# Graph layer over an 8192 x 8192 matrix: the cells for the row sums of stripe s+1 loaded among the pieces of stripe s, and a later column step

## What is computed

```python
h = jnp.maximum(_layernorm(x, axis=-1), 0.0)
A_hat = adj + jnp.eye(N)
d_inv_sqrt = jnp.sum(A_hat, axis=1) ** (-0.5)
A_norm = d_inv_sqrt[:, None] * A_hat * d_inv_sqrt[None, :]
out = x + relu(A_norm @ (h @ W.T))
```

## Time and profile before

| | |
|---|---|
| median of 3 runs | 1205.84 us (1203.95 to 1207.55) |
| span of the profiled execution | 1237.8 us |
| time of the profiled execution apart from its span | none is listed |
| PE / DVE / ACT busy | 983.2 / 802.4 / 586.5 us |
| moved by DMA | 391.81 MB, mean 317 GB/s |
| mean granted TensorE clock | 0.909 of full |

### The profile page before, as it was taken

How to read it: one execution, slowest core, us unless ns; L and a number is a source line. 1 busy time by engine, 2 the same in 40 slices (tenths; PEclk the granted TensorE clock), 3 DMA queues, 4 the chain that set the end, 5 groups by cost and what they waited for, 6 DMA issues and landing times.

```text
span 1237.8 us, 9242 instructions
## 1 busy us (share of the span) xinstructions
PE 983.2 (79%) x2365; PEld 451.8 (36%) x2365; DVE 802.4 (65%) x965; ACT 586.5 (47%) x1735; POOL 52.6 (4%) x61
## 2 busy tenths in 40 slices
PE   0633346566687788796597999999999999899997
PEld 0631122222233333342243444444444444344443
DVE  5342233444476566575485888888888888778775
ACT  2797587776384637145254451724715653010011
POOL 3000000000000000000000000000000000010001
PEclk9767668678889899998798999999999999999999
DMA  9989999999999999999999999999999997999993
GB/s 301 380 320 309 392 398 362 365 369 347 362 349 343 362 337 322 314 256 274 281 291 278 329 332 360 323 276 333 309 325 320 314 271 215 271 271 348 337 328 88
DMA packets 275204, 391.81 MB, mean 317 GB/s; under 512 B 10832, under 2 KB 252624, under 8 KB 275152
## 3 DMA queue, kind: packets, MB, share of 16 engines
q1 hardware_dynamic: 137648, 195.65, 51.3%
q10 hardware_dynamic: 137504, 195.58, 50.5%
HBM read 386.99 MB, written 4.19 MB: 316 GB/s over the span
## 4 chain that ended last, share of the span: by engine, by line
PE 37%; DMA 8%; ACT 6%; ACTq 3%; DVE 1%; issue 0%; POOLq 0%; SPq 0%; DVEq 0%
PE bank L485 36%; DMA slot<-in_adj_dram 8%; ACT junk L540 6%; ACTq L269 2%; DVE adjT L692 1%; ACTq L277 1%; PE pre L461 0%; ACTq L315 0%; DVE near L778 0%; ACT slot L530 0%; ACT near L558 0%; DVE part L677 0%; POOLq L175 0%; PE sums_bank L449 0%; ACTq L321 0%
## 5 line engine op out<-in xcount | busy, mean ns | idle before, releaser
L485 PE MATMUL bank<-adjT,support 128*128 128x512 f32 x2048 | 936.2, 618 | 152.1 <-DVE adjT L692 150.8
L692 DVE STREAM_TRANSPOSE adjT<-slot 128x1024 f32<-128x1024 f32 x450 | 546.5, 1233 | 268.8 <-DMA slot<-in_adj_dram 157.2
L485 PEld LDWEIGHTS bank<-adjT,support 128*128 128x128 f32 x2048 | 401.8, 199 | 664.6 <-issue 661.0
L540 ACT ACTIVATE junk<-slot 128x384 bf16<-128x384 f32 (+2 forms) x540 | 254.6, 473 | 196.1 <-issue 131.3
L530 ACT ACTIVATE slot<-slot 128x6144 f32<-128x6144 f32 (+11 forms) x64 | 191.8, 2998 | 250.3 <-issue 147.8
L558 ACT ACTIVATE near<-near,dinv 128x128 f32<-128x128 f32 x64 | 20.4, 390 | 177.9 <-issue 88.5
L540 ACT ACTIVATION_READ_ACCUMULATOR junk<-slot 128x1 f32 x540 | 100.8, 187 | 0.0
L692 DVE STREAM_TRANSPOSE adjT<-near 128x1024 f32<-128x1024 f32 x62 | 74.8, 1231 | 19.0 <-PE bank L485 19.0
L540 ACT ACTIVATE junk<-near 128x256 bf16<-128x256 f32 (+1 forms) x192 | 75.5, 394 | 2.8 <-ACT junk L540 2.8
L677 DVE TENSOR_REDUCE part<-slot 128x4 f32<-128x1536 f32 (+2 forms) x45 | 69.0, 1533 | 0.0
L407 POOL TENSOR_TENSOR dinv<-total,power 128x4 f32<-128x4 f32 x16 | 16.1, 1007 | 942.0 <-DVE total L746 942.0
(11 more groups left out here) (53 smaller groups left out, 179.1 us busy)
## 6 DMA issues: line engine op xcount, KB each, us to landing
slot<-in_adj_dram SPq DMA_DIRECT2D x118, 768.0 KB, 15.4
slot<-in_adj_dram ACTq DMA_DIRECT2D x118, 768.0 KB, 13.4
slot<-in_adj_dram ACTq DMA_DIRECT2D x56, 512.0 KB, 11.0
slot<-in_adj_dram SPq DMA_DIRECT2D x56, 512.0 KB, 12.0
slot<-in_adj_dram ACTq DMA_DIRECT2D x12, 1536.0 KB, 15.8
slot<-in_adj_dram SPq DMA_DIRECT2D x12, 1536.0 KB, 17.0
near<-in_adj_dram SPq DMA_DIRECT2D x30, 512.0 KB, 16.8
near<-in_adj_dram ACTq DMA_DIRECT2D x30, 512.0 KB, 15.2
```

Of the source, the lines that this page charges most:

```text
L485: ins = nc.tensor.matmul(bank[bank_of(g)][:], support[:, v * R + t, :], adjT[at % TURNS][:, r, :], start=(n == first_of[g] and t == 0), st ...
L540: nc.scalar.activation(junk[at % JUNKS][:, :n], cells[:, c, :], ACT.Copy, accum_out=part[u % 2][:, k, c:c + 1]).then_inc(junk_done, 1)
L692: nc.vector.transpose(adjT[at % TURNS][:].rearrange("p t (c i) -> p t c i", i=Q), half.rearrange("p c (t r) -> p t c r", r=Q)).then_inc(t_ ...
```

## The change

The four far pieces of stripe s+1 are no longer loaded at the head of stripe s+1. They are spread evenly over the pieces of stripe s: after the k-th of its own pieces (left, near, early), as many far pieces as make the share k of all. ACT sums them where they stand in the new list `stream[s]`. Three `far_sum` tiles replace two.

```diff
+    for u in range(NB):
+        stream[u], left[u], early[u] = [], [], []
+        if u == 0:
+            for piece_ in far_pieces(0):
+                place_piece(0, piece_)
+        own = [("left", u, v, n, 0, 0) for v, n in split(0, u)] + ["near"]
+        if u <= EARLY_TO:
+            own += [("again", i, u - MOST, MOST, 0, 0) for i in range(u - MOST - BAND - 1, -1, -MOST)]
+        ahead = far_pieces(u + 1)
+        done = 0
+        for k, piece_ in enumerate(own):
+            if piece_ == "near":
+                near_behind[len(landing) - 1] = u
+                stream[u].append("near")
+            else:
+                place_piece(u, piece_)
+            upto = len(ahead) * (k + 1) // len(own)
+            for piece_ in ahead[done:upto]:
+                place_piece(u, piece_)
+            done = upto
...
     for s in range(NB):
-        before = 0 if NB - 1 - s - BAND > 4 else min(FIRST, max(0, s - 1))
-        order += own[:before]
-        if s > 0:
-            column(s - 1)
-        order += own[before:]
+        lefts, behind = todo[s]
+        order += lefts[ready:]
+        following = todo[s + 1][0][:s] if s + 1 < NB else rest[:LEAD]
+        stripe_at[s] = len(order)
+        begun = behind[:LEAD]
+        ready = min(len(following), LEAD - len(begun))
+        order += begun + following[:ready]
+        column(s)
+        order += behind[LEAD:]
...
-        far_sum = [sb(f"far_sum{i}", [P, 2 * B]) for i in range(2)]
+        far_sum = [sb(f"far_sum{i}", [P, 2 * B]) for i in range(3)]
...
-                if m + AHEAD in last_piece:
-                    load_kept(act, (2, 3), last_piece[m + AHEAD])
+                if m + AHEAD in near_behind:
+                    load_kept(act, (2, 3), near_behind[m + AHEAD])
...
-            for s in range(NB + 1):
-                end = stripe_at[s + 1] if s < NB else len(order)
-                early = stripe_at[s] if s == 0 else min(column_at[s - 1], stripe_at[s] + 1)
-                for n in range(stripe_at[s], early):
-                    product(n)
-                if s > 0:
-                    fold_sums(s - 1)
+            for n in range(len(order)):
+                if folds < NB and n == min(stripe_at[folds] + 2, column_at[folds]):
+                    fold_sums(folds)
+                    folds += 1
+                product(n)
...
+            for s in range(NB):
+                fold_at.setdefault(min(stripe_at[s] + 2, column_at[s]), s)
+                totals_at.setdefault(min(stripe_at[s] + 3, column_at[s]), s)
+                scale_at.setdefault(min(stripe_at[s] + 4, column_at[s]), s)
```

More of the change, by code:

```diff
@@ L82, in gnn_kernel, with far_pieces @@
     landing = []
-    far, left, again, early = {}, {}, {}, {}
+    far, left, again, early, stream = {u: [] for u in range(NB)}, {}, {}, {}, {}
+    near_behind = {}
     next_cell = [u + BAND + 1 for u in range(FAR_ROWS)]
     middle = []
-    for u in range(NB):
+    def far_pieces(u):
         cells = NB - 1 - u - BAND
-        far[u] = []
         widths = [] if cells <= 0 else [cells] if cells <= MOST * B else [MOST * B, cells - MOST * B]
+        out_ = []
         for k, width in enumerate(widths):
@@ L91, in gnn_kernel @@
             per = min(B, MOST * B // width)
[L92 to L99, removed]
-        if u <= EARLY_TO:
[L101 to L105, removed]
+            out_ += [("far", u, bb, min(per, B - bb), NB - cells + k * MOST * B, width) for bb in range(0, B, per)]
@@ L128, in column, with cells_of @@
             order.append((i, s, None))
+    def cells_of(m):
+        u, v, n = landing[m][1:4]
+        return [(u, k, m) for k in range(v, v + n)]
+    todo = []
+    for u in range(NB):
+        lefts = [cell for m in left[u] for cell in cells_of(m)]
+        behind = [cell for m in early[u] for cell in cells_of(m)]
+        todo.append((lefts, behind))
+    rest = [cell for u in AGAIN_ROWS for m in again[u] for cell in cells_of(m)]
+    ready = 0
     for s in range(NB):
+        lefts, behind = todo[s]
+        order += lefts[ready:]
+        following = todo[s + 1][0][:s] if s + 1 < NB else rest[:LEAD]
         stripe_at[s] = len(order)
-        own = [(landing[m][1], v, m) for m in left[s] + early[s] for v in range(landing[m][2], landing[m][2] + landing[m][3])]
-        before = 0 if NB - 1 - s - BAND > 4 else min(FIRST, max(0, s - 1))
-        order += own[:before]
-        if s > 0:
-            column(s - 1)
-        order += own[before:]
[L138 to L142, removed]
+        begun = behind[:LEAD]
[3 more added lines that the diff above has]
+        order += behind[LEAD:]
+        if s + 1 == NB:
+            order += rest[ready:]
     place = {(u, v): n for n, (u, v, m) in enumerate(order)}
@@ L339, in done_by @@
             return sum(combined_at(k) + 1 < place[u, v + n - 1] for k in range(NB))
-        last_piece = {(far[u] + left[u])[-1]: u for u in range(NB)}
         @block.sync
@@ L487, in product @@
                     ins.then_inc(used, 1)
-            back = 0
-            for s in range(NB + 1):
-                end = stripe_at[s + 1] if s < NB else len(order)
-                early = stripe_at[s] if s == 0 else min(column_at[s - 1], stripe_at[s] + 1)
-                for n in range(stripe_at[s], early):
-                    product(n)
-                if s > 0:
-                    fold_sums(s - 1)
-                for n in range(early, end):
-                    product(n)
-                    if back < NB and n >= 4 + last_final(back):
-                        rows_back(back)
-                        back += 1
+            back = folds = 0
+            for n in range(len(order)):
[3 more added lines that the diff above has]
+                product(n)
+                if back < NB and n >= 4 + last_final(back):
+                    rows_back(back)
+                    back += 1
             while back < NB:
```

118 lines of the change are left out of this document (63 added, 55 removed).

## The result

The change costs 6%: median 1282.47 us over four executions (1272.1 to 1309.8) against 1206.69 over four of before (1203.95 to 1209.0), a ratio of 1.0607 [1.0539, 1.0675]. The execution of 1309.8 us counts as a slow one, and the ratio is taken without it. The direction was forecast; the size was +3.6 us and came out at +73 by the ratio, +76 by the medians.

A forecast was written before the change was run, and what follows sets the result against it. DMA was taken to bound the first phase, PE the last. Terms +19.2 - 6 - 6.9 - 2.7 = +3.6 us gave a span of 1241.4 from 1237.8, and a median of 1209.5, range 1190 to 1229.

The forecast's parts named there:

- the three reliefs: Stripes 10 and 11: no near-load wait (-6 us), two cells less behind the arrival (-6.9), no cold start (-2.7).
- Nothing is loaded less ... I cost it at nothing; what hides it is the full DMA.: Spreading far pieces loads the same bytes, so no cell reaches PE sooner; costed at nothing because DMA is full.
- my rivals: ACT as bound in stripes 6 to 8 (1224, 0.25); waits cost nothing (1190, 0.28); change does nothing (1206, 0.05).
- something comes back: Stripe 9's 271 GB/s stretch, named as where spreading could gain if full DMA did not hide it.
- The waits of ACT, the main term: ACT waits at near(3) to near(5) for late columns, DMA losing 2.6, 6.6 and 10 us: +19, bounds 8 and 34.
- The arrival at 675.40: End of DVE's wait for the load at stripe 11's start; said to set the end, with 155 cells behind it.
- The frame itself: After that arrival PE sets the time: 155 cells x 3.43 = 532 us, plus 30 us for restart, folds and tail.
- The wait of stripe 10: ACT's 9.2 us before the near load, behind column(9); its removal was forecast to give 6 us, bounds 0 and 9.2.
- The rest cost nothing: Third far_sum, moved folds, totals and fold_sums, and DVE's fold waits for ACT: nothing on the path.
- The second phase: From about slice 24 PE is full almost to the end, a cell costing it 3.43 us.
- ACT as the bound at 1224: Rival: ACT also becomes the bound in stripes 6 to 8, 5 us for each of three stripes; chance 0.25.

The follow-up runs named there:

- e1: Far pieces spread as in the change, but with the cell order of the kernel before: median 1361.22 us.
- e2: Cell order (late column) as in the change, but far pieces at the head of their own stripe as before: 1320.32 us, 1.0945.
- e18: e1 with two pieces in flight in place of three: 1271.86 us, 1.0519.
- e6: Loads alone, computation left out, in the changed kernel's spread load order, three pieces in flight: span 1170.3 us.
- e17: e6 with two pieces in flight in place of three: span 954.5 us.
- e4: The changed kernel with all near loads issued by GpSimd in place of SP and ACT: 1287.88 us, 1.0507.
- e3: The changed kernel, but up to stripe 6 only early cells, no left cells, may stand before the column: 1355.26 us, 1.1235.
- e11: e1 with a wait for all issued pieces to land in front of near(2) to near(10): 1279.53 us, 1.0598.
- e9: The kernel before, unchanged, profiled once more: 1204.63 us, span 1202.8.
- e12: The kernel before with one number changed, so that columns 9 and 10 stand at the head of their stripes: 1204.8 us, 0.9977.
- e8: Loads of the kernel before and its order up to column 8; from column 9 on the column behind up to five early cells: 1229.17 us, 1.0166.
- e13: The changed kernel up to column 8, with the order of the kernel before from column 9 on: median 1295.68 us (1257.58 to 1301.48).
- e10: e6 with a wait once a stripe, before the near load, until all issued pieces have landed: span 1041.0 us.
- e5: Loads alone, computation left out, in the load order of the kernel before, three pieces in flight: span 1077.3 us.

## Why the prediction was wrong

The sum failed in more than one term. The spans differ by 67.5 us where 3.6 were forecast, and the missing 64 divide as an account of the trace: 23 up to stripe 6, of which about 13 are slower packets and about 10 longer waits; 15.6 for the three reliefs, which did not come; 25 elsewhere, nearly all of it behind the start of stripe 8, costed at nothing. Of these the sizes are estimates; that the terms add up so is not shown, since e1 and e2 show that the two parts of the change do not add.

**The step that failed: "Nothing is loaded less ... I cost it at nothing; what hides it is the full DMA."** The byte count was right, and the conclusion took DMA's rate as a property of the piece (413, 346, 295 GB/s). It is one of the order and of how much is in flight as well. The spread order without the late columns costs 4 to 5% with two pieces in flight and about 155 us with three (e18, e1), and the loads without any computation show the fall with three and only a sag with two (e6, e17). None of my rivals had this mechanism, and no row of before shows it, except one that I passed over: stripe 9 with a share of 1.04 at 271 GB/s. I called it a place "where something comes back". It was the same thing, long packets, and asking what a busy DMA at 271 GB/s is doing would have raised the question.

**The waits of ACT, the main term.** The mechanism was right in kind: near(3), near(4) and near(5) waited as predicted, ACT idle before them for over 10 us, the rate below 250 behind it. Near(2), which the prediction does not follow at all, waited 18.4 us. The size was off twofold and outside the term's own bounds of 8 to 34.

| lag gained from (s,0) to (s+1,0) around near(s) | near(2) | near(3) | near(4) | near(5) | near(6) |
|---|---|---|---|---|---|
| predicted, us | 0 | 2.6 | 6.6 | 10 | 0 |
| measured, us | 3.4 | 8.3 | 11.3 | 16.9 | 2.3 |

The sum is 42.2 instead of 19.2. For 100 to 400 us the windows divide it: the rate is down by 13.6% (360 to 311), the share by 9.6% (1.04 to 0.94), and so the rest, some 4.4%, is slower packets. Of 300 us that is about 29 for a DMA without work and 13 for slower packets. So of the 23 us that were missing, about 10 are my arithmetic of the waits (near(2), costed at nothing, waited 18.4 us; near(5) 21.9), and 13 the term above. This division holds for the traces as they are; e4 shows that the 29 do not come back when the holes are filled. Against ACT's time the account also closes, as an estimate: it waits 76.7 us after and then issues in 1.55 each, 84.4 in all, where before it was held 37.7 us by five issues of 4.5 to 9.9 without a wait; the difference is 46.7, and the lag at (7,0) 44.1. What the Trainium skill (DMA: Bandwidth & Descriptors, Anatomy of one DMA) says, that the issuing sequencer does the waiting, is what these gaps show.

**Parts that do not add.** e2 puts the late column at +114 us and e1 the spread at +155; together they cost 75. The far pieces between near load and left piece shorten the wait (21.9 us at most, where e2 has 30.3), and the waits drain DMA once a stripe and keep its packets short. Taking them away (e3) costs 73 us; putting in idle ones (e11) gives 60 to 80. I had only the cost of a wait in the sum, not what DMA does after a pause.

**The reliefs, -6, -6.9 and -2.7, were not there; a new wait was.** The arrival at 675.40, on which all three stand, lies late by the disturbed part of that execution; its 32 us over the median were a warning that I explained and then did not heed, reading microseconds from inside the stretch that made them. The frame itself holds in e9: (11,0) is waited for 7.8 us and transposed at 641.6, and 641.6 + 532 + 30 is 1203.6 against a span of 1202.8. The wait of stripe 10 is there too, but it is not what makes that arrival late, since e12 takes it away for 2.8 us. And the late column brings in its own wait, which the prediction did not see: the last early cell now stands behind two column cells, its slot is released 6.9 us later, and the loads behind it wait (some 16 us in front of one issue of e8, 20 us in all for the kernel, 5 of them before stripe 8). I had followed what the near load waits for, but not what the other loads wait for when `order` moves. "The rest cost nothing" failed with it: the fold two cells behind the last left cell holds DVE for 9.1 and 6.0 us in stripes 10 and 11.

**The second phase.** PE is not hungry behind stripe 11 in either kernel, and the lag grows by only 7 us from there to the end, as the frame of the prediction has it. Its sums are right to within a microsecond (675.40 + 532 is 1207.4, not 1207.8). In the old load order e8, at 1229.17, stands at the range's upper end of 1229, with the late columns of stripe 9 and later alone; with those of the first stripes (e2) it is passed by 91 us.

The rival closest in sign, ACT as the bound at 1224, has the right engine for the wrong reason: ACT's share of the chain rises from 6 to 17%, but its busy time does not matter; it is what stands behind its waits.

**What stays open.** What makes the packets long, physically; it was shown to need no computation, to come in either order with three pieces in flight, and to be kept away by a pause once a stripe, but also to end without one. How the 17 us of stripes 8 to 11 divide: the rates of stripes 8 to 10 (335, 346 and 330 GB/s after, 349, 354 and 351 in e9, stripes of some 54 to 68 us) make about 9 as an estimate, slow packets and late slots together; the rest lies in the order of DVE's work, and e13 failed to separate them. Three near buffers would take the wait away without moving it to another queue; there was no space beside the slots, and that was not tried.

## What to carry to other kernels

Before a DMA's order is changed, find for each issuing engine what it waits for and what stands behind that wait; a wait before an issue costs only what it exceeds the time that the issue would block anyway. Read DMA's rate beside its share: a share above 1 at a falling rate is a trouble of its own, and what helped here was less in flight or a pause. And when a profiled execution is longer than the median, find the stretch that makes it so and take no price from inside it.

## What the runs showed of the hardware

More in flight can be slower. The same 333.52 MB in the same order, from one core, with no computation, one execution each:

| | span, us | lowest slice of the middle, GB/s |
|---|---|---|
| three pieces in flight (e6) | 1170.3 | 209 |
| three, drained once a stripe (e10) | 1041.0 | 261 |
| two pieces in flight (e17) | 954.5 | 287 |

Packets of 1536 bytes average 72 to 77 ns over 50 us in e9 between 300 and 700 us, and 99 to 115 in e1. In e6 they are long for hundreds of us, 99 to 120 ns from 250 to 700, and come back without a pause: 79 ns from 700 to 750, long again to 950, then 73 to 82. The old order with three in flight held out for some 400 us in e5 before it fell.

The issue of a near load (two DMAs) holds ACT for 4.5 to 9.9 us from near(2) to near(9) of e9, and for 1.5 where ACT has waited over 8 us in front of it, with DMA fully busy all the while.
